# A hybrid block on one core: small transfers placed elsewhere, a ring of four PSUM banks, and every fourth u*B on GpSimd

## What is computed

```python
delta = softplus(dt_in @ w_dt + b_dt);  A = -exp(A_log)
h = exp(dt[:, :, None] * A) * h + (dt * xt)[:, :, None] * bt[:, None, :]
y = einsum('bdn,bn->bd', h, ct)
```

## Time and profile before

| what | us |
|---|---|
| median of 3 runs | 1215.29 |
| lowest and highest run | 1210.8 and 1216.22 |
| the profiled execution | 1216.41 |
| its span, first to last instruction | 1214.6 |
| VectorE busy | 1071.7 |
| TensorE busy (matmuls) | 887.2 |
| GpSimd busy | 816.0 |
| ScalarE busy | 810.5 |

### The profile page before, as it was taken

One profiled execution on the slowest core, in us unless ns is written; L12 is line 12 of the kernel. 1 busy time (PEld: TensorE's weight loads), 2 busy tenths in 40 slices (PEclk: granted clock), 3 DMA queues, 4 the chain that ended last, 5 costly groups with the idle time before them and its releaser, 6 DMA issues. The chain is left out here.

```text
span 1214.6 us, 19663 instructions
## 1 busy us (share of the span) xinstructions
PE 887.2 (73%) x4292; PEld 364.4 (30%) x4292; DVE 1071.7 (88%) x2434; ACT 810.5 (67%) x2199; POOL 816.0 (67%) x558
## 2 busy tenths in 40 slices
PE   4286788687777786787767687768777777687775
PEld 1122333333323232332323233233332323232232
DVE  3389999989988999899989999898998899889993
ACT  4277784777746776578746877477775778556772
POOL 6466775767766776667766777576776677657663
PEclk9558898879886888878878989787988888888987
DMA  4543455434553444534454345543555434554430
GB/s 115 126 132 122 130 136 148 131 102 142 139 152 109 123 134 132 164 114 115 133 138 141 114 135 135 147 131 104 143 139 151 124 119 135 140 139 133 126 116 9
DMA packets 124133, 155.38 MB, mean 128 GB/s; under 512 B 32722, under 2 KB 57062, under 8 KB 124006
## 3 DMA queue, kind: packets, MB, share of 16 engines
q1 hardware_dynamic: 123494, 153.74, 45.7%
q0 software_dynamic: 512, 0.27, 0.2%
HBM read 137.63 MB, written 4.52 MB: 117 GB/s over the span
## 5 line engine op out<-in xcount | busy, mean ns | idle before, releaser
L1343 POOL TENSOR_TENSOR prod<-hst,C 128x1024 f32<-128x1024 f32 x256 | 603.9, 2359 | 337.2 <-DVE hst L1155 337.2
L1155 DVE TENSOR_TENSOR_SCAN hst<-bank,dbx 128x512 f32<-128x512 f32 x512 | 620.6, 1213 | 2.5 <-ACT bank L630 2.5
L630 ACT ACTIVATE bank<-wide,A_rep 128x512 f32<-128x512 f32 x512 | 351.6, 687 | 292.5 <-DVE hst L1155 274.1
L1149 DVE TENSOR_TENSOR dbx<-bank,B 128x512 f32<-128x512 f32 x512 | 344.6, 673 | 76.3 <-PE bank L875 70.8
L875 PE MATMUL bank<-spread,sel_bc 96*128 96x512 bf16 x512 | 216.2, 434 | 58.8 <-DVE dbx L1149 45.2
L644 ACT ACTIVATE prob<-s_sb,nmax 128x96 f32<-128x96 f32 x512 | 183.9, 360 | 0.0
L906 PE MATMUL bank<-k,q 128*128 128x384 f32 x256 | 133.2, 607 | 58.8 <-DMA k<-uv 37.2
L896 PE MATMUL bank<-prod,sel_red 128*32 128x512 f32 x1024 | 161.8, 709 | 4.4 <-POOL prod L1343 4.4
L913 PE MATMUL bank<-ident,prob 128*96 128x128 f32 x512 | 89.0, 303 | 63.9 <-ACT ao L660 61.3
L875 PEld LDWEIGHTS bank<-spread,sel_bc 96*128 96x128 bf16 x512 | 55.0, 108 | 201.7 <-DVE dbx L1149 119.1
L1348 POOL TENSOR_TENSOR prob<-prob,pinv 128x384 f32<-128x384 f32 x128 | 106.4, 831 | 9.8 <-DVE pinv L1176 7.6
(11 more groups left out here) (180 smaller groups left out, 915.2 us busy)
## 6 DMA issues: line engine op xcount, KB each, us to landing
wide<-dt_rows SPq DMA_DIRECT2D x512, 256.0 KB, 4.3
vw<-v_tok SPq DMA_DIRECT2D x80, 64.0 KB, 3.7
spread<-parts SPq DMA_DIRECT2D x96, 32.0 KB, 3.5
x_sb<-in_L_attn_x_dram SPq DMA_DIRECT2D x8, 256.0 KB, 4.4
dt_rows<-sp_t SPq DMA_DIRECT2D x8, 256.0 KB, 4.4
out_dram<-outb SPq DMA_DIRECT2D x8, 256.0 KB, 2.3
q<-qn SPq DMA_DIRECT2D x112, 16.0 KB
vw<-v_tok SPq DMA_DIRECT2D x16, 48.0 KB, 3.6
```

The costliest lines, as they stand in the source:

```text
L630: nc.scalar.activation(daP[s % 2][:, :], wide[m % SLOTS][:, s % 2, :], ACT.Exp, scale=A_rep[:, g:g + 1]).then_inc(exp_done, 1)
L1149: v.tensor_tensor(dbx[:, s % 3, :], uP[s % 2][:, :], B2[p][:, :], ALU.mult).then_inc(dbx_done, 1)
L1155: v.tensor_tensor_scan(hst[:, s % 4, :], daP[s % 2][:, :], dbx[:, s % 3, :], 0.0, ALU.mult, ALU.add).then_inc(scan_done, 1)
L1343: g.tensor_tensor(prod[:, 2 * (m % 4):2 * (m % 4) + 2, :], hst[:, 2 * (m % 2):2 * (m % 2) + 2, :], C2[p][:, :].unsqueeze(1).to_broadcast([ ...
```

## The change

Five things are changed together.

1. VectorE's multiplication by B is left out for q = 3 (`POOL_Q`), one unit in four. For these units u goes the way of dt: 32 rows of u are written to DRAM (`u_rows`), spread back by transfers of 256 KB into one of two `uwide` tiles (two per pair of groups, `widen_u`), and multiplied by B on GpSimd in place (`pool_input`), in iteration s with s % 4 = 1 for the group after. The matmul of `unit_u` and three of the twelve spread transfers go with it.
2. The two banks `daP` and the two banks `uP` become one ring of four banks, one per q. u of q = 0..2 is multiplied by B in its bank, and the tile `dbx` is gone; Exp writes back into `wide` for them. For q = 3 Exp writes into the fourth bank. TensorE fills the bank of unit s after the scan of unit s - 4, and still asks one unit ahead (`AHEAD` stays 1).
3. SP issues the next wide pair after the scans of the pair that used the tile, no longer after its Exp.
4. Places: the attention blocks start two iterations later, the job "k" is at 53 instead of 56 and "v" at 63 instead of 62. The parts are spread in three steps of three transfers at the pairs 18, 21 and 23, the values in four steps of three transfers at the pairs 0 to 3.
5. At the start of the kernel SP issues one part, one wide pair, the keys, the other three wide pairs and two uwide pairs, and ScalarE's queue issues the other two parts.

```diff
-          48: ("m", "es3"), 51: ("p", "q"), 52: ("m", "pt2"), 55: ("m", "pt3"), 56: ("p", "k"),
-          62: ("p", "v")}
+          48: ("m", "es3"), 51: ("p", "q"), 52: ("m", "pt2"), 53: ("p", "k"), 55: ("m", "pt3"),
+          63: ("p", "v")}
...
-PART_DMA_AT = {18: (0, 0), 19: (0, 2), 21: (1, 0), 22: (1, 2), 23: (2, 0), 24: (2, 2)}
+PART_DMA_AT = {18: 0, 21: 1, 23: 2}
...
-VALUE_DMA_AT = {0: (0, 0), 1: (0, 2), 2: (1, 0), 3: (1, 2), 4: (2, 0), 5: (2, 2)}
+VALUE_DMA_AT = {0: (0, 1, 2), 1: (3, 4, 5), 2: (6, 7, 8), 3: (9, 10, 11)}
...
-SCORES_AT = {33 * k // 10: k for k in range(NBLK)}
+SCORES_AT = {2 + 33 * k // 10: k for k in range(NBLK)}
...
+U_SLOTS = 2
+POOL_Q = 3
-N_PARTS_DMA = 12
+N_PARTS_DMA = 9
...
-        daP, uP, yP, sP, ptP, jobP = bank[0:2], bank[2:4], bank[4], bank[5], bank[6], bank[7]
+        uP, yP, sP, ptP, jobP = bank[0:4], bank[4], bank[5], bank[6], bank[7]
...
+        uwide = [sb(f"uwide{c}", [128, 2, L]) for c in range(U_SLOTS)]
-        dbx = sb("dbx", [128, 3, L])
...
+        def spread_parts(eng, B, p, part):
+
+            wait(eng, sp_step, B * N_SP + SP[("hi", "mid", "lo")[part]])
+            for c in range(POOL_Q):
+                eng.dma_start(spread[p][32 * part:32 * part + 32, c, :],
+                             parts[32 * c:32 * c + 32, part, :]).then_inc(parts_in, 16)
...
+                sp.dma_start(u_rows[p], uv[32 * POOL_Q:32 * POOL_Q + 32, :]).then_inc(urows_out, 16)
+
+            def widen_u(B, p, m):
+
+                wait(sp, scan_done, B * UNITS + 8 * (m - U_SLOTS) + 8)
+                if m == 0:
+                    wait(sp, urows_out, (B + 1) * 16)
+                flat = u_rows.rearrange("a d t -> (a d t)")
+                for j in range(2):
+                    row = p * 32 + 4 * m + j
+                    src = bass.AP(flat.tensor, flat.offset + row * L, [[0, 64], [2 * L, 2], [1, L]])
+                    sp.dma_start(uwide[m % U_SLOTS][64 * j:64 * j + 64, :, :], src).then_inc(uwide_in[m % U_SLOTS], 16)
 
             def widen(B, p, m):
 
-                wait(sp, exp_done, B * UNITS + 2 * (m - SLOTS) + 2)
+                wait(sp, scan_done, B * UNITS + 2 * (m - SLOTS) + 2)
...
+                    if m % 4 == 3:
+                        if m // 4 + U_SLOTS < GROUPS // 2:
+                            widen_u(B, p, m // 4 + U_SLOTS)
+                        elif not last(B):
+                            widen_u(B + 1, 1 - p, m // 4 + U_SLOTS - GROUPS // 2)
...
             def front(B, p):
                 store_rows(B, p)
-                for at in PART_DMA_AT.values():
-                    spread_parts(B, p, *at)
-                for m in range(SLOTS):
+                spread_parts(sp, B, p, 0)
+                widen(B, p, 0)
+                keys(B)
+                for m in range(1, SLOTS):
                     widen(B, p, m)
-                keys(B)
+                for m in range(U_SLOTS):
+                    widen_u(B, p, m)
                 load_weights()
...
-                wait(act, scan_done, B * UNITS + s - 1)
                 g = GROUPS * q + i
-                nc.scalar.activation(daP[s % 2][:, :], wide[m % SLOTS][:, s % 2, :], ACT.Exp,
+                to = wide[m % SLOTS][:, s % 2, :]
+                if q == POOL_Q:
+                    wait(act, scan_done, B * UNITS + s - 3)
+                    to = uP[q][:, :]
+                nc.scalar.activation(to, wide[m % SLOTS][:, s % 2, :], ACT.Exp,
                                      scale=A_rep[:, g:g + 1]).then_inc(exp_done, 1)
...
                 i, q = divmod(s, 4)
+                if q == POOL_Q:
+                    return
                 if s == 0:
                     wait(pe, parts_in, (B + 1) * 16 * N_PARTS_DMA)
-                wait(pe, dbx_done, B * UNITS + s - 1)
-                mm(uP[s % 2][:, :], sel_bc[:, i, :, :].rearrange("k j n -> k (j n)"), spread[p][:, q, :],
+                wait(pe, scan_done, B * UNITS + s - 3)
+                mm(uP[q][:, :], sel_bc[:, i, :, :].rearrange("k j n -> k (j n)"), spread[p][:, q, :],
                    start=True, stop=True).then_inc(u_ready, 1)
...
-                wait(dve, u_ready, B * UNITS + s + 1)
-                wait(dve, scan_done, B * UNITS + (s - 2 if s else 0))
-                v.tensor_tensor(dbx[:, s % 3, :], uP[s % 2][:, :], B2[p][:, :], ALU.mult).then_inc(dbx_done, 1)
+                i, q = divmod(s, 4)
+                if q == POOL_Q:
+                    return
+                wait(dve, u_ready, B * POOL_Q * GROUPS + POOL_Q * i + q + 1)
+                v.tensor_tensor(uP[s % 4][:, :], uP[s % 4][:, :], B2[p][:, :], ALU.mult).then_inc(dbx_done, 1)
 
             def unit_scan(B, s):
                 wait(dve, exp_done, B * UNITS + s + 1)
-                wait(dve, dbx_done, B * UNITS + s + 1)
+                i, q = divmod(s, 4)
+                if q == POOL_Q:
+                    wait(dve, gbx_done, B * GROUPS + i + 1)
+                    decay, into = uP[q], uwide[(i // 2) % U_SLOTS][:, i % 2, :]
+                else:
+                    wait(dve, dbx_done, B * POOL_Q * GROUPS + POOL_Q * i + q + 1)
+                    decay, into = wide[(s // 2) % SLOTS][:, s % 2, :], uP[q]
                 wait(dve, prod_done, B * PAIRS + s // 2 - 1)
-                v.tensor_tensor_scan(hst[:, s % 4, :], daP[s % 2][:, :], dbx[:, s % 3, :], 0.0, ALU.mult,
+                v.tensor_tensor_scan(hst[:, s % 4, :], decay[:, :], into[:, :], 0.0, ALU.mult,
                                      ALU.add).then_inc(scan_done, 1)
...
+            def pool_input(B, p, i):
+
+                if i == 0:
+                    wait(pool, done["p"], job_count("p", B, "B"))
+                if i % 2 == 0:
+                    wait(pool, uwide_in[(i // 2) % U_SLOTS], (B * (GROUPS // 2 // U_SLOTS) + i // 2 // U_SLOTS + 1) * 32)
+                u = uwide[(i // 2) % U_SLOTS][:, i % 2, :]
+                g.tensor_tensor(u, u, B2[p][:, :], ALU.mult).then_inc(gbx_done, 1)
...
+                    if s % 4 == 1:
+                        if s // 4 + 1 < GROUPS:
+                            pool_input(B, p, s // 4 + 1)
+                        elif not last(B):
+                            pool_input(B + 1, 1 - p, 0)
```

More of the change, by code:

```diff
@@ L202, in hybrid_block_kernel @@
         parts = sb("parts", [D, 3, L], BF16)
-        spread = [sb(f"spread{p}", [96, 4, L], BF16) for p in range(2)]
+        spread = [sb(f"spread{p}", [96, POOL_Q, L], BF16) for p in range(2)]
         dt_rows = nc.dram_tensor("dt_rows", [2, D, L], F32, kind="Internal").ap()
         wide = [sb(f"wide{c}", [128, 2, L]) for c in range(SLOTS)]
+        u_rows = nc.dram_tensor("u_rows", [2, 32, L], F32, kind="Internal").ap()
+        uwide = [sb(f"uwide{c}", [128, 2, L]) for c in range(U_SLOTS)]
         qn = sb("qn", [H * HD, L])
@@ L264, in hybrid_block_kernel @@
         wide_in = [sem(f"wide_in{c}") for c in range(SLOTS)]
+        urows_out, gbx_done = sem("urows_out"), sem("gbx_done")
+        uwide_in = [sem(f"uwide_in{c}") for c in range(U_SLOTS)]
         q0_in, q_in = sem("q0_in"), sem("q_in")
@@ L416, in body @@
                     if m in VALUE_DMA_AT and not first(B):
-                        window_values(B, *VALUE_DMA_AT[m])
+                        window_values(B, VALUE_DMA_AT[m])
                     if not last(B):
@@ L447, in load_weights @@
                 assert n == N_W_DMA
-            def spread_parts(B, p, part, c0):
-                wait(sp, sp_step, B * N_SP + SP[("hi", "mid", "lo")[part]])
-                for c in (c0, c0 + 1):
-                    sp.dma_start(spread[p][32 * part:32 * part + 32, c, :],
-                                 parts[32 * c:32 * c + 32, part, :]).then_inc(parts_in, 16)
             def keys(B):
@@ L461, in keys, with window_values @@
                         .then_inc(k_in, 16)
-            def window_values(B, j, m0):
+            def window_values(B, which):
                 wait(sp, done["p"], job_count("p", B, "v"))
-                for m in (m0, m0 + 1):
+                for j, m in (divmod(n, 4) for n in which):
                     blocks = [n for n in range(NBLK) if 0 <= n - 1 + j < NBLK and (n - 1 + j) % 4 == m]
@@ L618, in front @@
                     pre_job(name, B, p, front=True)
+                for part in (1, 2):
+                    spread_parts(act, B, p, part)
                 for s in range(AHEAD):
@@ L882, in front @@
                     pre_job(name, B, p, front=True)
-                unit_u(B, p, 0)
+                for s in range(AHEAD):
+                    unit_u(B, p, s)
             def y_start(B, p):
@@ L995, in body @@
                 for s in range(UNITS):
-                    if s < UNITS - 1:
-                        unit_u(B, p, s + 1)
+                    if s + AHEAD < UNITS:
+                        unit_u(B, p, s + AHEAD)
                     elif not last(B):
-                        unit_u(B + 1, 1 - p, 0)
+                        unit_u(B + 1, 1 - p, s + AHEAD - UNITS)
                     if first(B):
```

(1 more changed line is left out.)

4 lines of the change are left out of this document (2 added, 2 removed).

## The result

The changed kernel takes 1195.4 us (median of 4 runs, 1192.3 to 1201.2), the kernel before, on the same chip, 1215.1 us: ratio 0.985, 95% interval 0.981 to 0.990. Forecast were 1144 us. The direction was right; of 71 us expected 20 came.

A forecast was written before the change was run, and what follows sets the result against it. The prediction took VectorE to bound the kernel, busy 132.0 of 143.0 us a batch. Its terms, -74 + 20 - 18 - 7 + 12 - 5 + 1 = -71 us, gave 1145 from the profiled 1216.4, 1144 as median; range 1125 to 1165, chance 0.50.

The forecast's parts named there:

- Slots of VectorE, -74: VectorE's multiplications by B: 128 go, each freeing a slot of 0.58 us on the path, -74 us.
- +1: VectorE's softplus sum, slowed by a busier GpSimd: +1 us in all (0 to +4).
- GpSimd, +20: New waits behind GpSimd, which gets the fourth product u*B: 2.5 us a batch, +20 us (+5 to +60).
- Rival A: GpSimd becomes the bound, 138.5 us a batch: 1180 us, chance 0.20.
- Values and residual, -18: Value transfers issued earlier and wanted later, so the residual's wait behind them goes: -18 us (-20 to 0).
- Near unit 30, -7: VectorE's wait near unit 30, halved as probability copies shift against the softplus steps: -7 us (-14 to 0).
- Keys, +12: Batch start: keys land later, unit 4's multiplication waits 7.5 us against 4.1, partly hidden: +12 us for seven boundaries.
- rival B: Later scores cover half of today's key waits (-12, not +12), GpSimd's waits are 10, not 20: 1110 us, chance 0.18.
- DMA, "there is room: 0": DMA engines: 128 more loads raise the share from 0.54 to 0.72 at units 32 to 39, costing 0.
- Start, -5: Kernel start: spread transfers on two queues, keys before three of four wide pairs: -5 us (-10 to 0).
- Scans, D: Slower: a scan whose first operand is in SBUF shuts GpSimd out, +415 us, 1559 us, chance 0.05.
- rival C: No gain: VectorE's freed time returns as waits for TensorE, about 1215 us, chance 0.07.

The follow-up runs named there:

- e1: The changed kernel with GpSimd's multiplication u*B left out, its transfers kept (leaves work out, only to measure): 1182.9 us.
- e3: The changed kernel with the old places of keys, values and attention blocks: 1224.1 us.
- e6: The changed kernel with the output chain of the batch's end one unit later and the store one pair later: 1163.3 us.
- e4: The kernel before with the new places alone, without the ring of four banks or u*B on GpSimd: 1201.4 us.
- e16: e6 with the 128 uwide transfers left out, their semaphores passed on (leaves work out, only to measure): 1140.8 us.
- e2: The changed kernel with each u transfer cut to 1/32 of its bytes, as many transfers (leaves work out, only to measure): 1188.3 us.
- e13: The kernel before with the new places, the output chain one unit later and the query transfers issued by ScalarE: 1190.9 us.
- e11: e6 with the query transfers issued by ScalarE at units 56 to 62 instead of SyncE, nothing left out: 1139.5 us.
- e5: The changed kernel with the key transfers earlier, at pair 27 instead of pair 30 of SyncE's program: 1195.2 us.

## Why the forecast was wrong

- **Slots of VectorE, -74.** The slot of 0.58 us and the count held; busy time fell by 56.1. The step that failed is "+1" for instructions beside a busier GpSimd. The forecast looked at the one that was slow already, the softplus sum, which became faster by 11.2 us; the two of lines 1190 and 1127, with both operands in SBUF, stood among the fast ones and took 21.6 us more. The term that measured +15 with the setup's 5 stood in the sum as +1. Writing to PSUM in place, 0 in the sum, is 4 us at most.
- **GpSimd, +20.** Measured 8.9 us for products and 1.6 for u*B. Rival A is refuted by e1.
- **Values and residual, -18.** -20.0, right, but by the places alone: e3, ring and product without them, waits 49.7 us there. **Near unit 30, -7**: 12.3 us at unit 31 before, none after.
- **What the sum did not have at all.** The sum has for the new places only the waits that they ease, and not whom the shifted blocks meet. Block 11's norm meets `root2`: 26.1 us at unit 22 against 6.3, and e6 shows 32 us for the chain's place. Units 17 and 32 bring some 10 and 9 us more, in e4 too in part. This is the largest error.
- **Keys, +12.** VectorE's idle time at units 0 to 5 rose by 11 us in seven batches: the size was right, the picture wrong, so that is luck in part. TensorE's waits for keys fell, from 25.5 to 18.9 us, and of the 7.5 us forecast at unit 4 came 3.0 a batch (21.3 in seven). Left alone, the new places nearly clear the keys' waits (e4: 1.2 us a stage), and more than rival B had it, and the u transfers and the pace bring them back. I had priced two transfers at 1.2 us once, where the queue was already without a gap for 20 us; e16 prices all 128, issues and bytes, at 22 us.
- **DMA, "there is room: 0".** The mean share rose to 0.60, and e2 shows 7 us for the bytes.
- **Start, -5.** VectorE's waits between the first multiplication and that of unit 8 fell from 10.9 to 3.4 us, and the first multiplication came 1.9 us later: -5.6, and unit 8's multiplication starts at 64.42 us, not at 70.05. The size is right and the reason isn't: e4, with the new places and the old order of transfers, has it at 65.39.
- **Scans, D.** 1209 ns: refuted, for the reason given.

The busy part missed by 17 us and the idle part (+32 in place of +2) by 30; together 47, and the profiled run lies 3 us below its median. The forecast named the sign of this miss ("its idle time leaves 8 to 15 us a batch": 17.2), and gave rival C, that freed time returns as waits for TensorE, only 0.07. The price of ring and product by themselves was nearly right, once neither the chain nor SyncE's queue stood beside them: -74 + 20 - 5 + 1 = -58 us were forecast and -51 measured. From e13's profiled run to e11's, VectorE's busy time falls by 63.6 us (73 forecast) and its idle time rises by 14.5 us (15 forecast), the latter by other waits than those in the sum: its waits for products are 10.2 us, where 20 were forecast.

## What to carry to other kernels

When steps are moved in a hand-written order, list for each iteration what now meets on every in-order engine, not only the waits that the move eases. Here blocks that had moved by two iterations met the output chain, and moving that chain by one unit gave 32 us, where 128 multiplications less had taken 56 us from VectorE's busy time. Count a queue's issue time as an engine's busy time: where SyncE issues without a gap, each added transfer costs its 0.6 to 0.7 us and those behind it are late; a second queue helped here (24 us), another order (e5) didn't. And an edit whose gain seems lost may be worth nearly its full price behind the next cause: -9, 6, 29 and 51 us were the same edit.
